# A reordered opening and a row sum that ends on TensorE, in an attention and MLP block

## What is computed

```python
ada = silu(c) @ Wada.T + bada            # six vectors of D per batch
shift_msa, scale_msa, gate_msa, shift_mlp, scale_mlp, gate_mlp = split(ada, 6)
h = rmsnorm(x, g1) * (1 + scale_msa) + shift_msa
q, k, v = h @ Wqkv.T + bqkv              # per head: rmsnorm(q)*gq*hd**-0.5, rmsnorm(k)*gk
o = softmax(q @ k.T) @ v
x = x + gate_msa * (o @ Wproj.T + bproj)
h = rmsnorm(x, g2) * (1 + scale_mlp) + shift_mlp
x = x + gate_mlp * (gelu(h @ Wfc1.T + bfc1) @ Wfc2.T + bfc2)
```

## Time and profile before

| what | value |
|---|---|
| median of three runs | 1812.02 us (1808.69, 1813.46, 1812.02) |
| the profiled execution | 1810.62 us, of which 1808.8 us are the span of the trace |
| TensorE busy | 1727.9 us, 96% of the span |
| VectorE busy | 1085.6 us, 60% |
| ScalarE busy | 919.6 us, 51% |
| GpSimd busy | 372.5 us, 21% |
| first `qk` | 68.8 us after the span's start |
| last `row_sums` | at 981.3 us; the MLP follows |

### The profile page before, as it was taken

The page is one execution under the profiler, slowest core; times in us unless marked ns, Lnnn a source line. Parts: engine busy times, 40 slices in busy tenths (PEclk is TensorE's granted clock), DMA queues, the critical chain, the costliest instruction groups (busy, mean ns, idle before and its releaser), DMA issues.

```text
span 1808.8 us, 23247 instructions
## 1 busy us (share of the span) xinstructions
PE 1727.9 (96%) x8376; PEld 1154.5 (64%) x8376; DVE 1085.6 (60%) x1325; ACT 919.6 (51%) x1136; POOL 372.5 (21%) x305
## 2 busy tenths in 40 slices
PE   6998999999999999999889999999999999999998
PEld 3554555555555555554224787878788887878786
DVE  6678888898898898878788545142332324142301
ACT  4476666777777777778787432222221212221221
POOL 3001111100001000000140233333332333333332
PEclk8999999999999999999999899999999999999999
DMA  5754545555555555555765201010020202010000
GB/s 195 214 144 132 135 123 139 132 147 135 154 135 134 146 130 156 127 135 153 174 144 196 74 18 58 25 52 24 12 70 6 64 17 64 17 52 23 17 18 24
DMA packets 122242, 176.92 MB, mean 98 GB/s; under 512 B 29568, under 2 KB 43904, under 8 KB 121136
## 3 DMA queue, kind: packets, MB, share of 16 engines
q1 hardware_dynamic: 115952, 156.41, 32.3%
q10 hardware_dynamic: 5408, 16.81, 2.5%
q0 software_dynamic: 800, 2.62, 0.5%
HBM read 124.87 MB, written 50.92 MB: 97 GB/s over the span
## 4 chain that ended last, share of the span: by engine, by line
PE 44%; issue 29%; DVE 11%; POOL 9%; ACT 4%; DMA 2%; SPq 0%; POOLq 0%; ACTq 0%; DVEq 0%
PE scores L513 9%; PE pv L530 8%; PE gemm L588 7%; DVE sums L791 5%; PE scores L1303 5%; POOL act_parts L1235 5%; PE gemm L601 4%; ACT probs L704 3%; PE pv L1320 3%; PE gemm L1320 2%; PE aux L554 2%; POOL y L1233 2%; PE aux L547 1%; DVE raw L816 1%; DVE raw L862 1%
## 5 line engine op out<-in xcount | busy, mean ns | idle before, releaser
L704 ACT ACTIVATE probs<-scores,shift 128x1024 f32<-128x1024 f32 x512 | 548.7, 1113 | 195.4 <-PE scores L513 178.7
L791 DVE TENSOR_TENSOR sums<-sums,probs 128x2048 f32<-128x2048 f32 x192 | 453.8, 2363 | 32.7 <-ACT probs L704 28.0
L513 PE MATMUL scores<-q_stack,k_stack 128*128 128x512 f32 x1024 | 358.8, 435 | 6.3 <-ACT probs L704 6.1
L1303 PE MATMUL scores<-w_hi,act_parts 128*128 128x512 f32 x1024 | 318.7, 392 | 0.0
L513 PEld LDWEIGHTS scores<-q_stack,k_stack 128*128 128x128 f32 x1024 | 173.8, 189 | 202.3 <-issue 105.5
L1235 POOL TENSOR_TENSOR act_parts<-act_full,act_parts 128x512 fp32r<-128x512 f32 x128 | 172.5, 1348 | 514.2 <-ACT act_parts L1166 513.6
L530 PE MATMUL pv<-probs,v 128*32 128x512 f32 x2048 | 253.1, 603 | 0.4 <-ACT probs L704 0.4
L1303 PEld LDWEIGHTS scores<-w_hi,act_parts 128*128 128x128 f32 x1024 | 191.4, 189 | 38.8
L1303 PE MATMUL scores<-w_lo,act_parts 128*128 128x512 f32 x512 | 199.9, 391 | 0.0
L1373 DVE TENSOR_TENSOR y_next<-pv,p_bias 128x512 f32<-128x512 f32 x28 | 19.3, 691 | 299.7 <-PE pv L1275 299.7
L1166 ACT ACTIVATE act_parts<-act_full 128x512 fp32r<-128x512 f32 x128 | 80.9, 632 | 224.5 <-PE scores L1303 223.5
(11 more groups left out here) (167 smaller groups left out, 1944.1 us busy)
## 6 DMA issues: line engine op xcount, KB each, us to landing
k_stack<-parts_scratch SPq DMA_DIRECT2D x128, 256.0 KB, 5.0
q_stack<-parts_scratch SPq DMA_DIRECT2D x128, 256.0 KB, 5.1
parts_scratch<-parts SPq DMA_DIRECT2D x62, 512.0 KB, 2.9
inverse<-inverse_scratch SPq DMA_DIRECT2D x128, 64.0 KB, 2.1
heads_out<-o_out SPq DMA_DIRECT2D x32, 256.0 KB, 5.2
out<-result SPq DMA_DIRECT2D x32, 256.0 KB, 2.0
heads<-heads_out SPq DMA_DIRECT2D x28, 256.0 KB, 3.6
x_tile<-in_x SPq DMA_DIRECT2D x28, 256.0 KB, 2.8
```

The source lines that it names most:

```text
L513: mm = nc.tensor.matmul(scores[p][:, i, :], k_stack[s][:, h, j * P:(j + 1) * P], q_stack[half][:, h, :], start=True, stop=True)
L704: nc.scalar.activation(probs[L % RING][:, 2 * p:2 * p + 2, :], scores[p][:], ACT.Exp, bias=small["shift"][:]).then_inc(exp_done, 1)
L791: nc.vector.tensor_tensor(sums[:], a[:], probs[l % RING][:], ALU.add).then_inc(added, 1)
L1303: mm = nc.tensor.matmul(acc[t], act_parts[m % 2][:, b, t * P:(t + 1) * P], w2[a][:, m, :], start=(m == 0 and i == 0), stop=(m == NM - 1 an ...
```

## The change

- The modulation rows come first in the opening: both are moved out before ScalarE splits any weight, and the turn of the rows, the bias and the first modulated tiles move to earlier steps. VectorE's split of the v weights then stands behind `MOD_MADE` and the first modulated tile, where it stood ahead of them.
- The plan of the opening is v0, k, q, v1, v2, v3, v4, k, q in place of v0, v1, v2, k, q, v3, v4, v5, k, q. Product v5 moves to step 0; v6 takes step 1 and v7 step 2 (before: v6 in step 0, v7 in steps 1 and 2).
- The 4 MB of `ada_w` are issued on ScalarE's queue right behind the q, k, v weights, and `ADA_MM` comes one step earlier, ahead of the last `sum_squares` of the opening.
- For half-groups from `LEAN` = 26 on, VectorE makes six additions. `row_sums` waits for these, and then adds the eighth probability tile with four more matmuls by the ones matrix into the same bank. The counts of all waits on `added` follow, and ScalarE waits for `rs_mm` before it writes over the eighth tile's buffer.

```diff
-PLAN = placed(-18, 0, [v_of(0, 1), v_of(1, 1), v_of(2, 1), k_of(0, 0, 1), q_of(0, 0, 1), v_of(3, 1), v_of(4, 1), v_of(5, 1),
-                       k_of(0, 1, 1), q_of(0, 1, 1)])
+PLAN = placed(-18, 0, [v_of(0, 1), k_of(0, 0, 1), q_of(0, 0, 1), v_of(1, 1), v_of(2, 1), v_of(3, 1), v_of(4, 1), k_of(0, 1, 1), q_of(0, 1, 1)])
-PLAN += placed(0, 0, [v_of(6, 1), v_of(7, 2), k_of(1, 0, 2), ...
+PLAN += placed(0, 0, [v_of(5, 1), v_of(6, 1), v_of(7, 1), k_of(1, 0, 2), ...
-STAT = [-24, -23, -22, -21, -20, -19, -18, -17]
-NORM = [-23, -22, -21, -20, -19, -18, -17, -16]
-TURN = [-24, -23, -22, -21, -19, -18, -17, -16] + ...
-HOUT = [-19, -19, -18, -18, -17, -16, -15, -15]
+STAT = [-26, -25, -24, -23, -22, -20, -18, -16]
+NORM = [-25, -24, -23, -22, -21, -19, -16, -15]
+TURN = [-25, -24, -23, -22, -18, -17, -16, -15] + ...
+HOUT = [-22, -20, -21, -19, -17, -15, -14, -13]
-SPLIT = [-19, -18, -17, -16, -15, -14, -13, -12] + ...
+SPLIT = [-21, -20, -19, -18, -15, -14, -13, -12] + ...
-SPLIT_W = {"act": {-23: 0, -20: 1, -17: 2}, "dve": {-20: 0, -19: 1, -16: 2}}
-ROW_MM, ROW_MOVED, MOD_TURN, MOD_MADE, GAINS = {-25: 0, -24: 1}, {-24: 0, -22: 1}, -23, -20, -18
-ADA_LOAD, ADA_BIAS, ADA_MM, ADA_MADE, ADA_STORED = -14, -9, -8, -5, 2
+SPLIT_W = {"act": {-24: 0, -20: 1, -18: 2}, "dve": {-22: 0, -20: 1, -19: 2}}
+ROW_MM, ROW_MOVED, MOD_TURN, MOD_MADE, GAINS = {-27: 0, -26: 1}, {-26: 0, -25: 1}, -25, -23, -18
+ADA_BIAS, ADA_MM, ADA_MADE, ADA_STORED = -9, -10, -5, 2
...
+LEAN = -(-max(FILL) // NT)
+def adds_until(l):
+    hh, j = l // NT, l % NT
+    return ADDS * min(hh, LEAN) + (ADDS - 1) * max(0, hh - LEAN) + (min(j, ADDS - 1) if hh >= LEAN else j)
...
         def row_sums(hh):
-            pe.wait_ge(added, ADDS * (hh + 1))
+            pe.wait_ge(added, adds_until(NT * hh + NT - 1))
             aux_free()
             for h in range(HG):
-                mm = nc.tensor.matmul(aux[...], small["ones"][:], sums[:, h, :], start=True, stop=True)
+                mm = nc.tensor.matmul(aux[...], small["ones"][:], sums[:, h, :], start=True, stop=(hh < LEAN))
+            if hh >= LEAN:
+                l = NT * hh + NT - 1
+                pe.wait_ge(exp_done, 2 * l + 2)
+                for h in range(HG):
+                    mm = nc.tensor.matmul(aux[...], small["ones"][:], probs[l % RING][:, h, :], start=False, stop=True)
...
-                act.wait_ge(added, ADDS * (l // NT) + max(1, l % NT))
+                act.wait_ge(added, adds_until(l + 1 if l % NT == 0 else l))
+                if l // NT >= LEAN and l % NT == NT - 1:
+                    act.wait_ge(rs_mm, l // NT + 1)
...
         setup["scalar_first"](act)
+        for i in range(NA_LATER):
+            ...
+            act.dma_start(ada_w[i], ...).then_inc(ada_w_in[i], 16)
...
-            if L == ADA_LOAD:
-                (the same four loads)
...
         def add(l):
-            if j == 0:
+            if j == 0 or hh >= LEAN and j == NT - 1:
                 return
```

More of the change, by code:

```diff
@@ L82 @@
                k_of(2, 1, 3), v_of(7, 2), q_of(2, 1, 3), k_of(3, 1, 3), q_of(3, 1, 3)]
-START, AFTER_LAST = -25, 2
-PLAN = placed(-18, 0, [v_of(0, 1), v_of(1, 1), v_of(2, 1), k_of(0, 0, 1), q_of(0, 0, 1), v_of(3, 1), v_of(4, 1), v_of(5, 1),
-                       k_of(0, 1, 1), q_of(0, 1, 1)])
+START, AFTER_LAST = -27, 2
+PLAN = placed(-18, 0, [v_of(0, 1), k_of(0, 0, 1), q_of(0, 0, 1), v_of(1, 1), v_of(2, 1), v_of(3, 1), v_of(4, 1), k_of(0, 1, 1), q_of(0, 1, 1)])
 FIRST_PRODUCTS = len(PLAN)
-PLAN += placed(0, 0, [v_of(6, 1), v_of(7, 2), k_of(1, 0, 2), q_of(1, 0, 2), k_of(1, 1, 2), k_of(2, 0, 2), q_of(2, 0, 2),
+PLAN += placed(0, 0, [v_of(5, 1), v_of(6, 1), v_of(7, 1), k_of(1, 0, 2), q_of(1, 0, 2), k_of(1, 1, 2), k_of(2, 0, 2), q_of(2, 0, 2),
                       q_of(1, 1, 2), k_of(3, 0, 2), q_of(3, 0, 2), k_of(2, 1, 2), q_of(2, 1, 2), k_of(3, 1, 2), q_of(3, 1, 2)])
@@ L109 @@
 ROWS_AT, COMPACT_AT, INVERT_AT, INVERTED_AT, SPREAD_AT, OUT_AT = (at_row(x) for x in (ROWS, COMPACT, INVERT, INVERTED, SPREAD, OUT))
-STAT = [-24, -23, -22, -21, -20, -19, -18, -17]
-NORM = [-23, -22, -21, -20, -19, -18, -17, -16]
-TURN = [-24, -23, -22, -21, -19, -18, -17, -16] + [19, 21, 23, 27, 31, 35, 39, 45]
-HOUT = [-19, -19, -18, -18, -17, -16, -15, -15]
+STAT = [-26, -25, -24, -23, -22, -20, -18, -16]
+NORM = [-25, -24, -23, -22, -21, -19, -16, -15]
+TURN = [-25, -24, -23, -22, -18, -17, -16, -15] + [19, 21, 23, 27, 31, 35, 39, 45]
+HOUT = [-22, -20, -21, -19, -17, -15, -14, -13]
 for b in range(2, B):
@@ L119 @@
 HOUT += [step + 1 for step in TURN[NT:]]
-SPLIT = [-19, -18, -17, -16, -15, -14, -13, -12] + [step + 1 for step in HOUT[NT:]]
+SPLIT = [-21, -20, -19, -18, -15, -14, -13, -12] + [step + 1 for step in HOUT[NT:]]
 STAT_AT, NORM_AT, TURN_AT, SPLIT_AT = ({step: n for n, step in enumerate(table)} for table in (STAT, NORM, TURN, SPLIT))
@@ L543, in row_sums @@
         def row_sums(hh):
-            pe.wait_ge(added, ADDS * (hh + 1))
+            pe.wait_ge(added, adds_until(NT * hh + NT - 1))
             aux_free()
             for h in range(HG):
-                mm = nc.tensor.matmul(aux[h * DH:(h + 1) * DH, :], small["ones"][:], sums[:, h, :], start=True, stop=True)
+                mm = nc.tensor.matmul(aux[h * DH:(h + 1) * DH, :], small["ones"][:], sums[:, h, :], start=True, stop=(hh < LEAN))
+            if hh >= LEAN:
+                l = NT * hh + NT - 1
+                pe.wait_ge(exp_done, 2 * l + 2)
+                for h in range(HG):
+                    mm = nc.tensor.matmul(aux[h * DH:(h + 1) * DH, :], small["ones"][:], probs[l % RING][:, h, :], start=False, stop=True)
             mm.then_inc(rs_mm, 1)
@@ L715, in scalar @@
         setup["scalar_first"](act)
+        for i in range(NA_LATER):
+            cols = slice((NA_NOW + i) * CH, (NA_NOW + i + 1) * CH)
+            act.dma_start(ada_w[i], dram["wadaT"][:, cols].rearrange("(k p) n -> p k n", p=P)).then_inc(ada_w_in[i], 16)
         for L in range(START, AFTER):
@@ L724, in scalar @@
                 setup["scalar_split"](act, SPLIT_W["act"][L])
-            if L == ADA_LOAD:
-                for i in range(NA_LATER):
-                    cols = slice((NA_NOW + i) * CH, (NA_NOW + i + 1) * CH)
-                    act.dma_start(ada_w[i], dram["wadaT"][:, cols].rearrange("(k p) n -> p k n", p=P)).then_inc(ada_w_in[i], 16)
             if L == ADA_BIAS:
@@ L788, in add @@
             else:
-                dve.wait_ge(added, hh * ADDS + j - 1)
+                dve.wait_ge(added, adds_until(l - 1))
                 a = sums
```

## The result

| | before | after |
|---|---|---|
| median of 20 runs each | 1811.32 us (1808.69 to 1814.45) | 1814.74 us (1813.29 to 1818.09) |
| the profiled execution | 1810.62 us | 1816.38 us |
| first k product of step 3 | 79.86 us | 91.48 us |
| from there to the end of the span | 1728.9 us | 1723.1 us |

The ratio is 1.0021, with a 95% interval of 1.0014 to 1.0028. So the changed kernel is slower by 0.21%, inside the 0.3% that the prediction called no change. It forecast 1811.0 us, a change of -1.0 us. The time lies 3.7 us above that, near the upper end of the range (1815), and it moved the other way. The last two lines of the table split the change at step 3's k product: the opening costs 11.6 us, and everything behind it gains 5.8 us.

A forecast was written before the change was run, and what follows sets the result against it. It took the TensorE-ScalarE loop of scores and probabilities to set the pace in the last stretch, and TensorE's nearly gapless work the opening. Row sums -5.4 plus opening +4.4 made -1.0 us: median 1811.0, range 1803.5 to 1815.

The forecast's parts named there:

- The early load of 4 MB costs and gains nothing: Opening: the loads follow the q, k, v weights on their queue and nobody waited for the data, so 0 us.
- the fourth: Rival: the 4 MB slow SyncE's transfers, bada_cols and the biases, by up to 2 us; 1813 us, chance 0.07.
- The start and the first products: Opening: bias added at 21.65 us, v0 starts at 28.3, 0.75 us earlier; k and q follow, qk at 67.6 or 69.4.
- The early case: Opening: GpSimd does tile 3 before the q weights' split, ready at 35.5 us; qk at 67.6, opening costs 3.7 us.
- TensorE's wait ahead of k: Opening: TensorE finishes v0 and a turn at about 33.4 us, then stands 2.1 to 4.4 us for tile 3.
- Steps 0 to 3: Behind the opening's products: a bank wait and twelve more matmuls put step 3 16.0 us after qk, at 83.6 or 85.4.
- The wait ahead of v6: After qk: bias additions on VectorE delay the move of v5's bank, so TensorE waits 2.7 us.
- The row sums: Half-groups 26 to 31: removed waits and low clock give -10.7 us, added matmuls cost 5.3, together -5.4 us.
- the second rival: Half-groups 26 to 31: the stall stays, as weigh and ScalarE's move wait for the multiplication; 1821.7 us in full, chance 0.10.
- 6 x 0.89 = 5.3 us: Half-groups 26 to 31: four added matmuls delay weigh by 0.89 us each half-group, unhidden, 5.3 us in all.
- 0.7 us had been put on top of that case: Opening: cost put at +3.7 to +5.5 us, and 4.4 taken, nearer the early case.

The follow-up runs named there:

- e3: The kernel before with only the four 1 MB loads moved early on ScalarE's queue: 1815.67 us, ratio 1.0021 against before.
- e2: The changed kernel with the early 4 MB issued by SyncE behind qk_bias instead of ScalarE: 1809.03 us, ratio .9986 against before.
- e1: The changed kernel with the 4 MB loads back at their old late step, -14, on ScalarE's queue: 1811.17 us, ratio 1.0001 against before.
- e5: e2 with VectorE's four bias additions of the later modulation moved behind the move of v5's bank: 1804.93 us, ratio .9962 against before.
- e8: The kernel before with six additions in half-groups 26 to 31 and no added matmuls, the eighth tile left out: 1801.10 us, .9941 against before.
- e6: e5 with bada_cols issued behind the first tile of x, ahead of the other seven: 1802.83 us, ratio .9949 against before.
- e11: The changed kernel with one of the four early loads on ScalarE and three on SyncE: 1809.43 us, ratio .9992 against before.
- e10: e5 with the old order of products, ADA_MM at -9 and bada_cols issued behind the first x tile: 1803.67 us, ratio .9952 against before.

## Why the prediction came out as it did

**The step that failed** is "The early load of 4 MB costs and gains nothing". The argument was that the loads follow the weights on their own queue and that no one waits for the data. Both are true, and both miss the issuing engine: ScalarE stands in its own program until each transfer is taken, here until 24.3 us, and the modulation rows wait behind that. e3 shows the price alone (step 3 late by 5.15 us), and after against e2 shows it in the new order (91.48 - 86.69 = 4.8). In e2 the kernel takes 1809.03 us, for the 1811.0 of the forecast, and is faster than before (ratio .9986). The same edit also gains something that the sum did not have: e1 shows that with the loads left late, the new order pays 4.09 us ahead of `qk`, and has step 3 2.7 us later than e2. They had to move, but onto another engine.

**The rival that came nearest**, the fourth, had the right size (1813) and the wrong path. It had the 4 MB slow SyncE's transfers. `bada_cols` lands after 14.1 us in after, for 14.6 before. So it is luck that the time still lies in the range: its upper end was drawn for this rival.

**The start and the first products.** In e2, where ScalarE is free, the forecast can be held against the trace: bias 21.78 (21.65), v0 28.92 (28.3), k 36.34 (35.5), q 40.90 (40.3), `qk` 68.37 (67.6). The early case was the true one. TensorE's wait ahead of k is only 1.11 us (2.1 forecast), because v0 ran at a granted clock of 0.50 (28.90 to 33.90 us) and took 5.3 us, where the forecast took the 4.5 of the kernel before. The 0.6 us at v0 is a step that the sum left out: GpSimd's `x_inv` of one column came between the split and `h_lo`. It stands at 29.93 in after, 0.16 us behind VectorE's split at 29.77, and ends at 32.46, 0.41 us behind the split's end at 32.05. It took 2.53 us. The Trainium skill ("SBUF — State Buffer", section "Who interferes with whom") has the later of two such instructions blocked for the whole length of the first. The trace agrees, for an operand of 128 numbers too.

**Steps 0 to 3** were right in mechanism and too small. The wait ahead of v6 is 2.92 us (2.7). The sum did not charge the clock for it, though it charged 1.7 us for each of two waits of 3.45 and 3.10 us at the other end of the kernel. e5 puts that at 10.7 - 9.1 = 1.6 us. From `qk` to step 3 it is 18.3 us for 16.0: 0.2 of that is the wait, 1.6 the clock, and 0.5 is not assigned.

**The row sums** were right in sign and in mechanism: nothing came back on `sums`, and next to nothing on `o_done`. But the second rival was nearer than the forecast had it. `output` still waits for the spread reciprocals, 3.96 us in half-group 27 of after, and ends at 905.31 + 0.69 = 906.00. The `weigh` that needs it starts at 906.15, some 0.2 us late, and the row sums are 20.67 us apart there for 20.45. The term "6 x 0.89 = 5.3 us" was too large, at 4.4 us: 0.74 us each for 0.89. Part of the difference is this same multiplication: in e8, where no added matmul stands ahead of `weigh`, one `weigh` waits for it at 892.99, 1.25 us behind its row sum where 0.89 is usual.

**The sum again**, for the profiled execution: forecast -1.0 us, measured +5.8. ScalarE's block is 4.8 of the 6.8 us between them, the clock behind v6's wait 1.6, `x_inv` 0.6, and what lies behind step 3 gives back 0.4. The other steps of the opening come 0.9 us later than in the early case, of which 0.7 us had been put on top of that case, so 0.2 is left. The 0.4 is two things. From the row sum of half-group 25 to the end after gains 957.7 - (1814.6 - 863.25 = 951.35) = 6.4 us, 1.0 more than forecast. Between step 3 and that row sum, where no edit stands, it loses 0.6 (771.8 us for 771.2, and 769.9 to 772.3 in e1 to e6 and e8 to e11). The medians differ by only 3.4 us, so some 2.4 us of the 5.8 are the spread of single executions, and which stretch they belong to isn't settled.

## What to carry to other kernels

An early load is free only if the engine that issues it has nothing due: count the issue itself in that engine's program, and put large loads on an engine whose queue may stand. Before an instruction is moved ahead of another, ask what on the same engine is behind it in the new order: the bias additions ahead of v5's bank and the split of the q weights ahead of v0's bank each kept TensorE waiting for some 3 to 4 us, and one number in a table undid each. A change that is two changes should be timed as two. Here one gave 6.5 us and the other took more than that.

## What the hardware showed

- An issue of 1 MB takes 0.38 to 0.81 us when ScalarE's queue is empty, and 2.7 to 6.5 us right behind the 3 MB of the q, k and v weights (2.73 to 5.91 in after, 6.46 in e11). The profile counts this neither as busy nor as a DMA wait. It shows as ACTq in the chain, and as "issue" behind the next instruction's idle time. The Trainium skill ("Perfetto Trace Analysis", section "DMA Instruction — HWDGE (DVE, Sync)") says that the issuing sequencer is free for its next instruction only when all descriptors of the transfer have been generated, and the rows fit it: ScalarE's first move stands at 24.37 in after, right behind the end of the last issue at 24.32. Which limit the queue runs into isn't shown by any run: SyncE meets one as well, in the kernel before too, where the issue of the 4 KB `qk_bias` takes 4.48 us behind its loads of x.
- GpSimd's `x_inv`, on one column, took 2.53 us beside VectorE's split of a weight slice, and 0.56 us at 44.13 in after, away from any split.
- Behind a wait of 2.92 us TensorE's clock was down in after, e2 and e11, to a mean of 0.66 over the 5 us that followed, so part of them at the lower of its two levels. Behind waits of 3.52 us in e10 and 4.09 us in e1 it was 0.50 for all 5 us, and behind the 2.34 us ahead of k in after it stayed at 1.00. The first kind cost 1.6 us (e5), and the second, by an estimate from its rows, at least 5 x 0.50 = 2.5 us.
